# A graph network on one Trainium2 core: edge slots in seven groups of 512 destinations in place of five of 640, and a recurrent layer with one register load per tile and two casts on ScalarE

## The reference

```
h[dst] += x[src]                                           # 1: a scatter-sum
repeat 10: f += max over edges with edge_src = n of
           relu(f[edge_dst] - f[edge_src]) * sqrt(weight)  # 2: an infinity norm
for l in 3 layers: agg = sum of nw * x[src] per dst, then
           gates I, F, T, O of agg @ W, out = O * tanh(C)  # 3: recurrent layers
m = MLP(x_i, x_j - x_i), mean of m per dst                 # 4: an edge network
```

## Time and profile before

| what | value |
| --- | --- |
| median of 3 runs | 9872.44 us (9860.09 to 9875.16) |
| the profiled execution: its own time | 9882.23 us |
| its span | 9880.4 us |
| mean granted TensorE clock in it | 0.92 of full speed |
| PE, DVE, ACT, POOL busy | 71%, 76%, 38%, 37% of the span |
| bytes moved | 1233.55 MB, mean 125 GB/s |

### The profile page before, as it was taken

One profiled execution on the slowest core, in us unless ns is written; L12 is line 12 of the kernel. 1 busy time (PEld: TensorE's weight loads), 2 busy tenths in 40 slices (PEclk: granted clock), 3 DMA queues, 4 the chain that ended last, 5 costly groups with the idle time before them and its releaser, 6 DMA issues. The chain is left out here.

```text
span 9880.4 us, 145528 instructions
## 1 busy us (share of the span) xinstructions
PE 7018.8 (71%) x43605; PEld 3615.3 (37%) x44075; DVE 7488.9 (76%) x12160; ACT 3767.0 (38%) x4241; POOL 3639.5 (37%) x3081
## 2 busy tenths in 40 slices
PE   3101399980779797978879797978687888846665
PEld 2101255540334343433334343433344444423332
DVE  8878788862678787878778787877898989954443
ACT  0000066650445454545545454545122212213333
POOL 0047788881233242423333232333000000047775
PEclk9999999995899999999999998999899999977777
DMA  2000011116767676767667676766211111111111
GB/s 82 3 11 5 6 41 39 41 35 219 236 211 239 205 245 205 244 206 234 216 204 241 203 244 201 244 205 222 58 58 46 58 44 60 56 18 29 27 27 26
DMA packets 593293, 1233.55 MB, mean 125 GB/s; under 512 B 128487, under 2 KB 241975, under 8 KB 592418
## 3 DMA queue, kind: packets, MB, share of 16 engines
q1 hardware_dynamic: 263170, 851.76, 26.9%
q10 hardware_dynamic: 231360, 335.60, 9.3%
q0 software_dynamic: 97984, 36.11, 3.0%
HBM read 992.41 MB, written 231.17 MB: 124 GB/s over the span
## 5 line engine op out<-in xcount | busy, mean ns | idle before, releaser
L1449 PE MATMUL acc<-dst_hot,parts 128*128 128x512 bf16 x11130 | 2878.5, 382 | 953.4 <-issue 697.1
L1508 ACT ACTIVATE parts_out<-acc 96x1024 bf16<-96x1024 f32 x2320 | 2316.5, 1019 | 2273.5 <-PE acc L1460 1762.6
L1413 POOL DMA_INDIRECT group_best<-best_dram,best_row x1250 | 1457.1, 1166 | 3163.2 <-SPq L1379 2787.5
L1338 DVE TENSOR_SCALAR dst_hot<-dst_rows,node_f 128x2048 bf16<-128x2048 int16 x2910 | 2050.1, 740 | 178.9 <-PE acc L1460 147.0
L1449 PEld LDWEIGHTS acc<-dst_hot,parts 128*128 x11600 | 1048.3, 97 | 2208.0 <-issue 968.7
L907 POOL DMA_INDIRECT gathered<-table_dram,gather_index x830 | 960.6, 1157 | 2067.9 <-POOLq L156 1807.5
L298 POOL DMA_INDIRECT got_src<-edges_dram,gather_index x928 | 1166.1, 1257 | 851.0 <-DVEq L746 559.9
L1800 DVE TENSOR_SCALAR dst_hots<-node_row,dst_col 128x640 bf16<-128x640 int16 x2784 | 931.5, 383 | 54.7
L1460 PE MATMUL acc<-source,parts 128*128 128x128 bf16 x9280 | 910.0, 221 | 5.3 <-issue 0.8
L1751 PE MATMUL sums_by_dst<-dst_hots,edge_message 128*96 128x512 bf16 x2784 | 880.0, 392 | 22.5 <-DVE dst_hots L1800 9.3
L1006 PE MATMUL acc<-hot_space,parts 128*96 128x512 bf16 x3828 | 858.7, 380 | 42.4 <-DVE hot_space L931 42.4
(11 more groups left out here) (363 smaller groups left out, 7248.9 us busy)
## 6 DMA issues: line engine op xcount, KB each, us to landing
dst_rows<-step_dst_dram SPq DMA_DIRECT2D x582, 512.0 KB, 4.6
source<-source_dram SPq DMA_DIRECT2D x582, 512.0 KB, 7.8
best_dram<-best_out ACTq DMA_DIRECT2D x580, 256.0 KB
factor<-slot_weight_dram ACTq DMA_DIRECT2D x560, 256.0 KB
sources<-source_dram SPq DMA_DIRECT2D x174, 512.0 KB, 3.3
joined<-slot_inside_dram ACTq DMA_DIRECT2D x560, 64.0 KB
dst_rows<-step_src_dram SPq DMA_DIRECT2D x58, 512.0 KB, 5.9
source_dram<-source SPq DMA_DIRECT2D x58, 512.0 KB, 6.8
```

The source lines that it names most:

```text
L1338: nc.vector.tensor_scalar(hot[k % 2][b][:, :], index_rows[k % 3][:, :], node_f[:, b:b + 1], None, ALU.is_equal).then_inc(hot_ready, 1)
L1413: pool.indirect_dma_start(group_best[:, g, h, :], None, best_dram, bass.IndirectOffsetOnAxis(ap=best_row[:, i:i + 1], axis=0)).then_inc(en ...
L1449: nc.tensor.matmul(acc[n % 3][:, 0:TILE], blocks[b], hot[k % 2][b][:, q * TILE:(q + 1) * TILE], start=(b == 0), stop=(b == DST_BLOCKS - 1))
L1508: act.activation(moved[n % (2 * QUADS)][:, :], acc[n % 3][0:SPLIT, :], ACT.Copy).then_inc(tile_moved, 1)
```

## The change

Groups hold 4 blocks (512 destinations) in place of 5 (640): 7 groups, 175 buckets and 61 steps (244 tiles, 976 slot columns) in place of 5, 125, 58 (232, 928). The last group holds the one block that is left. The keys would no longer fit their bits, so they get a signed form (`key_bits`, `key_of`); the order of the buckets is worked out with each group's own size. The loop of layer 2 has four one-hots and four 512-column matmuls per tile, not five. The recurrent layers have one 512-column matmul per 128 slots in place of 512 + 128 columns, one load of the tile's number, used for both addresses, and the two casts of the messages go to ACT, between its moves; DVE then waits for them at stages 4 and 7. Not shown: the buffers, the sizes that follow, and the cutting of `sums` for the gates, which has two pieces per group of columns as before.

```diff
-DST_BLOCKS = 5
-DST_GROUPS = HI // DST_BLOCKS
+DST_BLOCKS = 4
+DST_GROUPS = -(-HI // DST_BLOCKS)
-TILE, QUADS, STEPS1 = BANK, 4, 58
+TILE, QUADS, STEPS1 = BANK, 4, 61
...
 def expected_step(i):
-    first, last = (b * (E // BUCKETS + P // 2) // TILE for b in (i, i + 1))
+    of_group = [min(DST_NODES, N - g * DST_NODES) * E // (N * HI) + P // 2 for g in range(DST_GROUPS)]
+    ahead = [HI * sum(of_group[:b // HI]) + b % HI * of_group[b // HI] if b < BUCKETS else HI * sum(of_group) for b in (i, i + 1)]
+    first, last = (a // TILE for a in ahead)
     return last % STEPS1 if first // STEPS1 == last // STEPS1 else STEPS1
...
+        def key_bits(link, to, key, below):
+            V = nc.vector
+            link(V.tensor_scalar(below, key, float(KEY_ZERO), -1.0, ALU.is_lt, ALU.mult))
+            link(V.tensor_scalar(to, key, -float(KEY_ZERO), None, ALU.add))
+            link(V.tensor_tensor(to, to, below, ALU.bitwise_xor))
+            link(V.tensor_scalar(to, to, float(KEY_BIAS), None, ALU.add))
+            link(V.tensor_scalar(to, to, ID_BITS, None, ALU.logical_shift_left))
+            link(V.tensor_scalar(below, below, 31, None, ALU.logical_shift_left))
+            link(V.tensor_tensor(to, to, below, ALU.bitwise_or))
...
-                    link(nc.vector.tensor_scalar(group_key, group_key, KEY_BIAS, None, ALU.add))
+                    key_bits(link, group_key, group_key, below[0:EP, :])
...
-                    def key_of(to, of):
-                        link(V.tensor_scalar(of, of, ID_BITS, None, ALU.logical_shift_right))
-                        link(V.tensor_scalar(to, of, -float(KEY_BIAS), float(BUCKETS * P - 1), ALU.add, ALU.min))
+                    def key_of(of):
+                        below = key_below[0:of.shape[0], 0:of.shape[1]]
+                        link(V.tensor_scalar(below, of, 0.0, -1.0, ALU.is_lt, ALU.mult))
+                        link(V.tensor_scalar(of, of, 1, ID_BITS + 1, ALU.logical_shift_left, ALU.logical_shift_right))
+                        link(V.tensor_scalar(of, of, -float(KEY_BIAS), None, ALU.add))
+                        link(V.tensor_tensor(of, of, below, ALU.bitwise_xor))
+                        link(V.tensor_scalar(of, of, float(KEY_ZERO), float(BUCKETS * P - 1), ALU.add, ALU.min))
...
-                        FINDS = (range(0, 4), range(4, 6), range(6, 7), range(7, 9))
+                        FINDS = (range(0, 4), range(4, 6), range(6, 8))
...
-                            for b in range(3 if k < STEPS1 else 0):
+                            for b in range(2 if k < STEPS1 else 0):
                                 hot_block(k, b)
                             rise_by_weight(k - 2)
                             if k < STEPS1:
-                                hot_block(k, 3)
+                                hot_block(k, 2)
                             scan_best(k - 2)
                             if k < STEPS1:
-                                hot_block(k, 4)
+                                hot_block(k, 3)
                             turn_best(k - 2)
...
-                                        nc.tensor.matmul(to[0], message[c % 2][:, i, :], dst_hot[n % HOTS2][:, 0:BANK], start=False, stop=False)
-                                        nc.tensor.matmul(to[1], message[c % 2][:, i, :], dst_hot[n % HOTS2][:, BANK:DST_NODES], start=False, stop=False).then_inc(added, 1)
+                                        nc.tensor.matmul(to, message[c % 2][:, i, :], dst_hot[n % HOTS2][:, :], start=False, stop=False).then_inc(added, 1)
+                                    if m + 1 < TILES:
+                                        if j == 0:
+                                            load_number(m + 1)
+                                            sources = sources_of(m + 1)
+                                        else:
+                                            for a in sources[2 * (j - 1):2 * j]:
+                                                pe.lower_ap(a)
...
+                        def cast(c, i):
+                            if not 0 <= c < STEPS1:
+                                return
+                            act.wait_ge(weighed_ready, 2 * c + i + 1)
+                            if not i and c >= 2:
+                                act.wait_ge(added, (c - 1) * STEP_SUBS)
+                            act.activation(message[c % 2][:, :, i * D:(i + 1) * D], weighed[c % 2][:, :, :], ACT.Copy).then_inc(part_ready, 1)
+                        for m in range(TILES + QUADS):
                             k, q = divmod(m, QUADS)
+                            if q == 2:
+                                cast(k - 1, 0)
+                            if q == 3:
+                                cast(k - 1, 1)
...
-                            elif stage == 3:
-                                if k >= 2:
-                                    dve.wait_ge(added, (k - 1) * STEP_SUBS)
-                                link(V.tensor_copy(to[:, :, 0:D], t))
                             elif stage == 4:
-                                link(V.tensor_tensor(t, t, to[:, :, 0:D], ALU.subtract))
-                            elif stage == 5:
-                                link(V.tensor_copy(to[:, :, D:2 * D], t))
-                            elif stage == 6:
+                                dve.wait_ge(part_ready, 2 * k + 1)
+                                V.tensor_tensor(t, t, to[:, :, 0:D], ALU.subtract).then_inc(weighed_ready, 1)
+                            elif stage == 7:
+                                dve.wait_ge(part_ready, 2 * k + 2)
                                 V.tensor_tensor(to[:, :, 2 * D:SPLIT], t, to[:, :, D:2 * D], ALU.subtract).then_inc(message_ready, 1)
```

More of the change, by code:

```diff
@@ L217, in program @@
             node_id = sb("node_id", [P, HI], I32, own)
+            below = sb("below", [P, EF], I32, own)
             keys = [sb(f"keys{o}", [P, SORT], I32, own) for o in range(2)]
@@ L452, in program @@
             fill_shifted = sb("fill_shifted", [P, FILLS], I32, own)
+            fill_below = sb("fill_below", [P, FILLS], I32, own)
+            key_below = sb("key_below", [P, PER], I32, own)
             bucket_key = sb("bucket_key", [P, BUCKETS], F32, own)
@@ L1721, in bank @@
                             return sums[0:SPLIT, i * BANK:(i + 1) * BANK]
-                        for i in range(DST_GROUPS + 1):
-                            for r in range(BANK // P):
-                                h = i * DST_BLOCKS + r if i < DST_GROUPS else (r + 1) * DST_BLOCKS - 1
-                                at = BEFORE - r * P
-                                nc.tensor.matmul(bank(i), own_rows(h), identity16[:, at:at + BANK], start=(r == 0), stop=False)
-                        nc.tensor.matmul(bank(DST_GROUPS + 1), own_rows(HI - 1), identity16[:, BEFORE:BEFORE + BANK], start=True, stop=False)
+                        for h in range(HI):
+                            i, r = divmod(h, DST_BLOCKS)
+                            at = BEFORE - r * P
+                            nc.tensor.matmul(bank(i), own_rows(h), identity16[:, at:at + BANK], start=(r == 0), stop=False)
+                        load_number(0)
+                        sources, to_next = sources_of(0), None
                         for k in range(STEPS1 + 2):
@@ L1831, in _ @@
                                     make_messages(k - 1, i // 2)
-                        dve.wait_ge(closed, DST_GROUPS + 2)
+                        dve.wait_ge(closed, DST_GROUPS)
                         def by_root(to, of, g):
```

102 lines of the change are left out of this document (56 added, 46 removed).

## The result

The changed kernel takes 10,275.7 us in the median of 4 runs (10,274.0 to 10,281.2), the kernel before 9,873.0: a ratio of 1.041, with a 95% interval of 1.039 to 1.043. It is slower by 403 us; forecast were 323.

What follows compares the result with a forecast made beforehand. It took four full DMA engines to bound layer 2 and DVE the recurrent layers. 142 + 371 - 190 = +323 us on 9882 gave 10,205, less 10 for the runs' median 10,195; range 10,100 to 10,290 (82%).

Steps and rivals of the forecast that it cites:

- +371: Layer 2, ten iterations: +37.1 us each for three more steps, 50 more fetches and a longer end; bounds 30 to 41.
- What bounds the loop: Layer 2: transfers set the 6.96 us step, with the loads of factor and joined on 4 full DMA engines.
- The rival that PE and DVE bound the loop: Layer 2: engines set the pace, transfers follow; step 5.65 us, -34 us per iteration, time 9485; chance 6%.
- Lighter PE and DVE work is worth nothing there: Layer 2: one one-hot and four matmuls fewer per step cost at nothing, because the transfers hide them.
- Three steps at 6.96 us, +20.9 per iteration: Layer 2: three more steps, each at the old step time set by transfers that stay byte for byte the same.
- The other terms of the iteration, 16.2: Layer 2, per iteration: +5.4 us for fetches of maxima, +8.8 for fetches held to the end, +2.0 for maxima over groups.
- 5.4 for the fetches: Layer 2: 50 more fetches of maxima at 0.108 us each on the full engines, +5.4 us per iteration.
- The sign that the prediction gave, 92 weight loads in 40 us: Layer 2: later windows of an iteration would hold 92 weight loads, 16 per step, which is 6.96 us a step.
- The tail, +8.8 and +2.0: End of a layer 2 iteration: seven more fetches held for the last steps, +8.8 us; two more maxima over groups, +2.0.
- Preparation, +142: Before layer 2: histogram +44 us, keys and comparisons +11, 48 record fetches +77, stored one-hots +10; bounds 115 and 160.
- The recurrent layers, -190: Three layers: DVE's step falls from 9.27 to 7.75 us, -63 us per layer; bounds -225 and -100.
- the 0.2 kept for waits on ACT: Recurrent layers: 0.2 us per step allowed for ACT's queued casts and moves, making the 7.5 us step 7.75.

Runs made afterwards that it cites:

- after_five: Changed kernel with the first 512-column matmul of each tile made twice and a fifth, unread one-hot of DVE per step in layer 2: 10,279.2 us.
- after_pe5: Changed kernel with the first of the four 512-column matmuls per tile of layer 2 made twice, so PE has five as before: 10,275.3 us.
- after_58b: Changed kernel with 58 steps in place of 61, run a second time: 9,940.3 us, a ratio of 1.007 to the kernel before.
- before_61b: Kernel before with 61 steps in place of 58, one-hot buffers taken by the step within the iteration: 10,420.8 us, a ratio of 1.055.

## Why the prediction was right, by its steps, and where a term was off

**The time came into its range partly by luck.** Forecast were +323 us and at most 10,290; measured are +403 and 10,275.7. Layer 2 alone came out at +509 where +371 was forecast, 49.8 per iteration where the prediction's own bounds were 30 to 41. Had the other two parts come as forecast, the time would have been near 10,330, outside the range. The recurrent layers (40 us better, just beyond their bound of -225) and the preparation (24 better) made up for nearly half of the miss.

**What bounds the loop: right, and now shown.** Four full DMA engines, read off the falling pace, the waits for `joined` and the long issues. Spreading the two loads takes off 717 and 375 us, and the counts of packets and the stretches with four engines at work show them directly. The rival that PE and DVE bound the loop is out: two versions with more work per step take the same time.

**Lighter PE and DVE work is worth nothing there: right.** `after_five` puts all of it back, and the time differs by 4 us, less than a measurement can tell.

**Three steps at 6.96 us, +20.9 per iteration: too small, and the term that was off.** In the kernel before they cost 37.9 (478.7 - 440.8). I took the pace of the late windows as fixed by the bytes. It isn't: the whole iteration's mean step went from 6.79 to 7.12. The other terms of the iteration, 16.2, measure 11.9 on top of that (490.6 - 478.7). This one term makes the forecast of layer 2 too small, by 17 us in each of ten iterations, of which 4 come back from the others. The same without an order of the two edits: from first to last tile +42.8 us were measured, forecast were 20.9 for the steps and 5.4 for the fetches. The sign that the prediction gave, 92 weight loads in 40 us, didn't come either: 86 in the mean.

**The tail, +8.8 and +2.0: somewhat large.** From the last source matmul to the maxima 34.3 us (mean of ten), before 29.2; from the maxima to the next tile 21.3 against 19.2. Together +7.2. The seven fetches more are there: when PE ends its last tile POOL has 17 left before and 25 after (means of ten). But they don't lengthen the end one for one. Before, the last 12 of them began 12 us behind PE, after a wait of 4.87 us; in the second iteration of the changed kernel POOL works off 25 in a row, 1.36 us apart in the mean, beginning as PE ends:

```profile
3572.08 1.44 POOL L1435 DMA_INDIRECT group_best<-best_dram,best_row  x1 [5.91 <-SPq L1401]
...
3604.60 0.94 POOL L1435 DMA_INDIRECT group_best<-best_dram,best_row  x1 [0.30 <-issue]
...
3606.98 7.15 DVE L1593 TENSOR_TENSOR cross_best<-cross_best,group_best 128x800 f32<-128x800 f32 x7 [17.24 <-DMA group_best<-best_dram,best_row]
```

**Preparation, +142: 118.5.** Up to the first record fetch 656.1 - 600.5 = 55.6, forecast 44 + 11. The 48 more fetches cost 50.7, not 77: the fetches themselves took what was assumed, 1295 + 305 ns beside the first layer, but POOL's gathers between them took 1076 ns each where they had taken 1288, 23 us over 108 of them. The stored one-hots +5.3, not 10. Not foreseen: the 6.2 us of the copy in the last section.

**The recurrent layers, -190: -230.** The step is 7.56, not 7.75: the 0.2 kept for waits on ACT weren't needed. This is the lower bound that the prediction named, -225, to within 5. With 640 destinations the casts leave 0.12 a step over the computed 8.07.

**The granted clock** in layer 2 fell from 0.95 to 0.90. It cost nothing: `after_pe5` had most of it back (0.93) for no gain. The prediction didn't speak of it.

## What to carry to other kernels

A mean DMA share of 0.7 can hide four engines that are full: where a pace falls inside a loop at full clock and the engine that starts transfers stands at an issue for microseconds, look at the outermost dimension of each transfer's pattern before anything is taken off the compute engines. Price more steps under a full resource by a run, not by the last windows' pace: it moved by 5% with no byte changed. And split a change before judging it: here the casts were worth 183 us, the smaller groups with their three more steps cost more than three times that.

## What the runs showed of the hardware that I had not expected

**A prime number of rows copied by one engine.** The copy of the destinations into the order of steps has the number of steps as its outermost dimension. While it is the only transfer, the DMA share and the GB/s (last two numbers) are, of before and `after_58b`, both with 58 steps, then of `before_61b` and the changed kernel, both with 61:

```profile
2502.50:2505.50 3.00, 0.00 (x0) 0.00 (x0) 0.00 (x0) 0.00 (x0) 0.00 (x0) 0.50 0.14 49
2549.00:2553.00 4.00, 0.00 (x0) 0.00 (x0) 0.00 (x0) 0.00 (x0) 0.00 (x0) 0.50 0.14 51
```

```profile
2568.00:2571.00 3.00, 0.00 (x0) 0.00 (x0) 0.00 (x0) 0.00 (x0) 0.00 (x0) 0.50 0.07 26
2621.00:2623.00 2.00, 0.00 (x0) 0.00 (x0) 0.00 (x0) 0.00 (x0) 0.00 (x0) 0.50 0.07 26
```

Two engines of 16 would be a share of 0.125, one 0.06. DVE's wait for the first rows that come of the copy is 18.5 and 18.7 us with 58 steps and 24.4 and 24.7 with 61, whatever the groups, for 232 and 244 KB. By the same section of the Trainium skill as above ("DMA: Bandwidth & Descriptors", "Why a DMA increments its semaphore by 16 and not by 1"), 58 = 2 x 29 would run on 2 engines and 61 on 1; the rows agree. No run changed that copy alone.

**The same bytes at different paces.** With the same bytes per step the mean step with four full engines was 6.79, 7.02, 7.12 and 7.16 us in four kernels. Neither the engines' load (7.16 with all of it put back) nor 50 fetches fewer (7.11) explains it.

**Fetches by POOL.** A gather of 128 rows took 1.29 us in one kernel and 1.08 in the other in the same place of the program, 108 of them, with nothing in the change that touches it. It goes with the number of steps, not with the groups: 1.08 us with 61 in `before_61b`, 1.28 with 58 in `after_58b`. Why isn't known. The lines view beside the first layer, of before, then of the changed kernel:

```profile
L907 POOL DMA_INDIRECT gathered<-table_dram,gather_index x108 | 139.1, 1288 | 32.9 <-issue 32.9
```

```profile
L929 POOL DMA_INDIRECT gathered<-table_dram,gather_index x108 | 116.2, 1076 | 32.9 <-issue 32.9
```
